# Degrees of a block by thirteen wide products and a masked sum, in the spread stage of a graph network kernel

## Chip, cores and metric

One core of a Trainium2 chip runs the whole program. The metric is device time in microseconds (us), from one launch. Engines: PE is TensorE (PEld its weight loads), DVE is VectorE, ACT is ScalarE, POOL is GpSimd, SP is SyncE, which here issues most DMAs.

## What is computed

Two graph layers on 6250 nodes and 206250 edges (100000 drawn ones in both directions and a self-loop per node, sorted by destination), each followed by a layer norm of the sum with its input. The first is attention with edge attributes and four heads of 64; the second is a pair of graph convolutions whose norm comes from the degrees:

```python
x = _layernorm(x + _L0_gnn_ref(x, edge_attr_64, W, att, bias, gamma, beta, edge_index))
# second layer, twice gcn_conv, then relu; x_out = _layernorm(x + that)
h = x @ W
deg = segment_sum(ones, dst, num_segments=n)
dinv = where(deg > 0, rsqrt(deg), 0.0)
norm = dinv[src] * dinv[dst]
out = segment_sum(h[src] * norm[:, None], dst, num_segments=n) + b
```

The degree of a node is the number of edges that end in it.

## The kernel before

The kernel is a row of stages, each a block of five instruction streams (one for each engine) that meet only in semaphores. The stage of this case is `spread_stage` (L734). It walks over the edges in 202 steps of 1024 edges (128 partitions, K = 8 each). Four steps make a block b, s = 0 to 3 is the step in it, and each has its own row buffer `rows[s]` (NR_BUF = 4). A step does two things.

*Edge rows.* PE turns the step's edge attributes in `turned` (`turn`, L1137), ACT copies them to SBUF (`evacuate`, L1089), PE multiplies them with the weights and adds a window of the source table (`product`, L1168 and L1174, in two halves), ACT takes the softplus (L1078, L1081), DVE weights the result with the attention vector and sums it up (`multiply` L1010, `add_up` L1019). Beside that, PE counts for every edge how many with the same block of source nodes stand before it (`count`, L1153 and eight products of L1156 into the bank `psr`, 450 columns and then 400, 350 and so on down to 50), and DVE turns these ranks into row numbers (`rank`, L967 to L978). POOL then writes the step's 1024 rows to DRAM, by eight indirect DMAs (`scatter`, L914): four when the first half's dot products are there, four when the second's are and when the next step's first product half is (`pre_ready[0]`, L918).

*Dense counts.* For the first 196 steps (blocks 0 to 48), the stage also builds the adjacency counts that the convolutions use. Each step handles a quarter of a block's destination lanes in four pieces q: DVE makes one-hots of columns (`columns`, L988) and lanes (`lanes`, L996), PE multiplies them (`adj`, L1185, three products of 392 columns), and ACT copies the sum to `cnts[u]` (`keep`, L1071). `cnts[u]` has 128 source lanes as partitions, and 49 chunks of 128 destination lanes; two of them alternate by block (u). At the end of a block ACT stores it with one DMA of 1568 KB.

The degrees of the 128 nodes of block b - 1 are the sum of its counts over source lanes and chunks. They are formed in block b. PE does it in `count` for step 1 of block b (`closes(b, s)`), ahead of the counting products: 49 products, one for each chunk, with the chunk as weights and one column of ones as the moving side, accumulated into one column of `psr`. `deg_ready` then lets DVE copy that column to `deg` (L972), in the middle of `rank` for step 1. ACT's first `keep` of a block waits for `deg_ready` too, since it writes the buffer that the degree products of one block earlier read.

PE's order in a step is written out by hand in `body` (L1189): adj 0, product half 0, adj 1, product half 1, turn of the next step, adj 2, count of the next step, adj 3. DVE's order (L1022): rank with columns and lanes of piece 1 in between, piece 2, one-hots and window mask of the next step, piece 3, multiply and add_up of both halves with the next step's piece 0 in between.

Of the kernel before, what the change touches and what calls it, by code (L numbers as in the profile page):

```python
# [15 lines left out]
fp32 = mybir.dt.float32  # L16
bf16 = mybir.dt.bfloat16
i32 = mybir.dt.int32
ALU = mybir.AluOpType
# [3 lines left out]
P = 128  # L23
# [22 lines left out]
CODE = 1024  # L46
TURN = 512
WIDE = 4
EXACT = 256
RANGE = 60.0  # L50
fp16 = mybir.dt.float16
# [682 lines left out]
def spread_stage(nc, z, m, sb, ps, sem, ea, att):  # L734
# [4 lines left out]
    with ExitStack() as ctx:  # L739
# [32 lines left out]
            "oh_ready", "ohT_made", "ranked", "summed", "idx_ready", "turned_ready", "evacuated"))  # L772
        pre_ready, exp_done, out_ready = ([sem(ctx, f"{n}S{h}") for h in range(2)] for n in (
            "pre_ready", "exp_done", "out_ready"))
        deg_ready = sem(ctx, "deg_ready")
        stored = [sem(ctx, f"adj_stored{u}") for u in range(2)]
        filled = sem(ctx, "filled_second")
        cut = z.groups[0] // NR_BUF
# [153 lines left out]
        def _(eng):  # L932
# [19 lines left out]
            def rank(b, s, h, between):  # L952

                t = step(b, s)
                j = s % 2
                count = Count()

                def own(ins, k):

                    ins.then_inc(v, count.up() and 1)  # L960
                    between(k)
                    eng.wait_ge(v, t * steps + count.n)

                wait(eng, sent[s], b * 16 * K)
                eng.tensor_copy(rows[s][:, :, LO:DOT], m["ends"][:, span(t * K, K), :])
                eng.wait_ge(ranked, t + 1)
                own(eng.tensor_tensor(  # L967
                    ranks[:, :, :], psr[:, 0:K * HB].rearrange("p (k h) -> p k h", h=HB),
                    m["base"][:, h, None, :].to_broadcast([P, K, HB]), ALU.add), 0)
                if closes(b, s):  # L970
                    eng.wait_ge(deg_ready, b)
                    eng.tensor_copy(m["deg"][:, span(b - 1, 1)], psr[:, (K + 1) * HB:(K + 1) * HB + 1])  # L972
                eng.tensor_tensor(m["base"][:, h, :], m["base"][:, h, :],
                                  psr[:, K * HB:(K + 1) * HB], ALU.add).then_inc(summed, 1)
                own(eng.tensor_tensor(ranks[:, :, :], ranks[:, :, :], oh[j][:, 0:K, :], ALU.mult), 1)
                assert count.n == steps
                with nc.allow_low_precision(reason="one whole number under 2**24 in each sum"):
                    eng.tensor_reduce(idx[s][:, :], ranks[:, :, :], AX.X, ALU.add).then_inc(idx_ready, 1)  # L978
# [36 lines left out]
            def add_up(b, s, part):  # L1015
# [3 lines left out]
                eng.tensor_reduce(rows[s][:, part * n:(part + 1) * n, DOT:DOT + DOTS], weighed[part][:, :, :, :], AX.X,  # L1019
                                  ALU.add).then_inc(dotted[part], 1)  # L1020

            def body(b, s, h=1):  # L1022
                nxt = later(b, s, 1)

                def between(k):
                    if dense(b):
                        (columns, lanes)[k](b, s, 1)

                rank(b, s, h, between)
                if dense(b):  # L1030
                    adj(b, s, 2)
                if exists(*nxt):
                    hots(*nxt)
                    windows(*nxt)
                if dense(b):
                    adj(b, s, 3)
                multiply(b, s, 0)
                if dense(nxt[0]):
                    columns(*nxt, 0)
                add_up(b, s, 0)  # L1040
                multiply(b, s, 1)
                if dense(nxt[0]):
                    lanes(*nxt, 0)
                add_up(b, s, 1)
# [4 lines left out]

            for j in range(2):  # L1050
                eng.memset(oh[j][:, K, :], 0.0).then_inc(cleared, 1)
            hots(0, 0)
            windows(0, 0)
            adj(0, 0, 0)
# [76 lines left out]
        def _(eng):  # L1131
            def turn(b, s):
                t = step(b, s)
                eng.wait_ge(ea_in[s % 2], ea_landed(b, s))
                wait(eng, evacuated, t)
                for g in range(K // 2):
                    mm = eng.transpose(turned[:, g, :], eaS[s % 2][:, 2 * g:2 * g + 2, :].rearrange("p k d -> p (k d)"), m["ident"][:, :])  # L1137
                mm.then_inc(turned_ready, 1)

            def count(b, s, u):  # L1140
                j = s % 2
                t = step(b, s)
                eng.wait_ge(oh_ready, t + 1)
                wait(eng, summed, t)
                if closes(b, s):
                    for q in range(GQ):
                        eng.wait_ge(copied[q], t - 1)
                    for c in range(NB):
                        mm = eng.matmul(psr[:, (K + 1) * HB:(K + 1) * HB + 1],
                                        cnts[1 - u][:, c, :, :].rearrange("p g d -> p (g d)"), m["onesb"][:, 0:1],  # L1150
                                        start=(c == 0), stop=(c == NB - 1), skip_group_check=True)
                    mm.then_inc(deg_ready, 1)
                eng.matmul(psr[:, 0:(K + 1) * HB], m["tri"][:, :], oh[j][:, :, :].rearrange("p k h -> p (k h)"),  # L1153
                           start=True, stop=False, skip_group_check=True)
                for d in range(1, K + 1):
# [5 lines left out]
            def product(b, s, h):  # L1161
# [13 lines left out]
                                        win[j][0:PW, :], start=False, stop=True, skip_group_check=True)  # L1175
                mm.then_inc(pre_ready[h], 1)

            def adj(b, s, q):
                t = step(b, s)
                r = q % 2  # L1180
# [8 lines left out]
            def body(b, s, u=None, after_u=1):  # L1189
# [9 lines left out]
                if u is not None:  # L1199
                    adj(b, s, 2)  # L1200
                if exists(*nxt):
                    count(*nxt, (after_u if u is None else u if s < NR_BUF - 1 else 1 - u))
                if u is not None:
                    adj(b, s, 3)

            def one(b, u):
                for s in range(NR_BUF):
# [5 lines left out]

            eng.wait_ge(cleared, 2)
            turn(0, 0)
            count(0, 0, 0)
            rounds(eng, NB // 2, two)
            if NB % 2:
                one(NB - 1, 0)
# [1913 lines left out]
```

## Time and profile before

| | us |
|---|---|
| median of 3 runs | 6543.93 |
| lowest and highest of them | 6538.44, 6555.55 |
| the profiled execution | 6502.53 |
| its span, first to last instruction | 6500.8 |
| spread stage in it, about | 301 to 3013 |

Over the whole span PE is busy 74%, DVE 75%, ACT 61%, POOL 62% of the time; the mean granted TensorE clock is 0.886 of full speed. The profiled execution is 41.4 us below the median of the runs. Stages follow each other with a barrier between them, so a us less in one stage is a us less in all. In the views below, "idle before" is the time in which the engine did nothing ahead of an instruction, followed by what ended it: an instruction of another engine, a DMA, "issue" (no semaphore update ended it) or "remote" (a semaphore update at whose time no sender's record ends).

### The profile page before, as it was taken

What the parts mean: (1) busy time and instruction counts of PE and PEld (TensorE: products, weight loads), DVE (VectorE), ACT (ScalarE), POOL (GpSimd) and SP (SyncE); (2) the same over time, 40 slices, a digit from 0 to 9 for tenths busy, and PEclk for the clock granted to TensorE, in tenths of its full rate; (3) what the DMA queues carried; (4) which work ended last, traced back from release to release, by engine and by line L of the source; (5) the groups of instructions that cost most, each with busy time, mean ns of one, the idle gap of its engine ahead of it and who ended that gap; (6) DMA issues with size and microseconds to landing.
All of it is one profiled execution on the core that took longest, in us unless ns stands there. A gap on an engine that the chain in (4) does not pass through costs nothing. (4 is left out here: it accounts for less than half of the span.)

```text
span 6500.8 us, 161934 instructions
## 1 busy us (share of the span) xinstructions
PE 4790.6 (74%) x32887; PEld 3107.1 (48%) x32888; DVE 4860.5 (75%) x21938; ACT 3979.7 (61%) x10577; POOL 4009.3 (62%) x5381
## 2 busy tenths in 40 slices
PE   1466666666666666664999999999938888886699
PEld 0233344334343433432555555555525556554699
DVE  6577777777677777773999999999976677777333
ACT  3355555555455545543999999999967777776100
POOL 1277777777677777764666666666627777776000
PEclk8588888878788778876999999999969999998799
DMA  8755556556455555555333333333317777775698
GB/s 224 239 186 182 186 193 197 184 191 194 160 188 174 175 170 167 176 162 160 72 72 72 72 73 74 73 73 73 73 37 216 217 217 223 213 219 174 258 360 344
DMA packets 1161941, 1090.82 MB, mean 168 GB/s; under 512 B 750004, under 2 KB 1023523, under 8 KB 1142980
## 3 DMA queue, kind: packets, MB, share of 16 engines
q1 hardware_dynamic: 1033656, 684.89, 38.9%
q0 software_dynamic: 88560, 320.26, 13.2%
q10 hardware_dynamic: 39580, 84.01, 3.4%
q8 instruction: 57, 0.93, 0.1%
q14 instruction: 88, 0.72, 0.0%
HBM read 658.14 MB, written 430.64 MB: 167 GB/s over the span
## 5 line engine op out<-in xcount | busy, mean ns | idle before, releaser
L914 POOL DMA_INDIRECT rows<-rowS,idx x1616 | 1949.0, 1206 | 787.9 <-issue 441.0
L1185 PE MATMUL psa<-one_c,one_s 128*128 128x392 bf16 x2352 | 605.1, 372 | 762.8 <-DVE one_s L996 461.4
L2425 PE MATMUL psm<-msg,onem 128*128 128x260 f32 x3648 | 918.0, 395 | 205.9 <-issue 169.7
L1694 DVE CUSTOM_DVE_ANT_0 junk<-bufh,attb 128x64 bf16<-128x64 f32 x5472 | 1043.5, 238 | 14.1 <-ACT bufh L1742 6.4
L2346 POOL TENSOR_TENSOR msg<-oj,heads 128x512 f32<-128x512 f32 x760 | 799.3, 1074 | 208.7 <-DMA oj<-rows 176.3
L988 DVE TENSOR_TENSOR one_c<-ioc,pairS 128x1176 bf16<-128x1176 f16 x784 | 598.4, 763 | 433.4 <-remote 227.7
L2425 PEld LDWEIGHTS psm<-msg,onem 128*128 128x128 f32 x3648 | 649.6, 190 | 474.0 <-issue 397.7
L1078 ACT ACTIVATE lgS<-preS 128x1024 f32<-128x1024 f32 x404 | 413.4, 1023 | 617.4 <-PE preS L1174 268.3
L1071 ACT ACTIVATE cnts<-psa 128x392 bf16<-128x392 f32 x784 | 366.8, 490 | 661.2 <-remote 344.3
L1782 PE MATMUL pre<-P3h,oneT 128*128 x5472 | 757.0, 275 | 0.0
L1659 POOL TENSOR_SCALAR one<-io128b,side 128x128 bf16<-128x128 bf16 x912 | 695.7, 763 | 67.2 <-DMA side<-rows 41.0
L2358 ACT ACTIVATE dist_m<-io,sums_lanes 128x128 f32<-128x128 f32 x1368 | 499.1, 396 | 292.4 <-PE psm L2425 265.1
L1185 PEld LDWEIGHTS psa<-one_c,one_s 128*128 128x128 bf16 x2352 | 211.0, 106 | 966.4 <-DVE one_s L996 640.4
L1667 POOL COPY eaC<-side 128x128 f32<-128x128 f32 x912 | 293.5, 322 | 572.0 <-PE turned L1769 565.7
L1777 PE MATMUL pre<-W2d,eaTh 64*128 64x256 f32 x3648 | 641.9, 429 | 0.0
L1782 PEld LDWEIGHTS pre<-P3h,oneT 128*128 128x128 bf16 x5472 | 460.9, 98 | 345.2 <-issue 303.0
L1738 ACT ACTIVATE lg<-pre 128x512 f32<-128x512 f32 x912 | 545.1, 598 | 111.2 <-PE pre L1782 110.5
L1168 PE MATMUL preS<-W2d,eaT 64*128 64x256 f32 x3232 | 590.0, 486 | 21.2 <-issue 19.0
L1742 ACT ACTIVATE bufh<-lg 128x512 f32<-128x512 f32 x912 | 574.6, 630 | 29.0
L1699 DVE CUSTOM_DVE_ANT_1 junk<-bufh,attb 128x128 bf16<-128x128 f32 x1824 | 560.6, 307 | 0.0
L2400 DVE TENSOR_TENSOR acc<-acc,psm 128x260 f32 x912 | 381.1, 418 | 108.3 <-DVE acc L2400 68.5
L1168 PEld LDWEIGHTS preS<-W2d,eaT 64*128 64x128 f32 x3232 | 346.3, 229 | 236.0 <-issue 201.4
(306 smaller groups left out, 9392.0 us busy)
## 6 DMA issues: line engine op xcount, KB each, us to landing
oj<-rows SPq DMA_DIRECT2D x912, 256.0 KB
adj<-adj SPq DMA_DIRECT2D x70, 1568.0 KB, 9.7
adj<-cnts ACTq DMA_DIRECT2D x49, 1568.0 KB
side<-rows SPq DMA_DIRECT2D x912, 69.0 KB, 2.3
bufh<-rows SPq DMA_DIRECT2D x912, 64.0 KB, 2.3
eaS<-in_edge_attr_dram SPq DMA_DIRECT2D x201, 256.0 KB
low<-dlow SPq DMA_DIRECT2D x202, 252.0 KB
adj_early<-adj SPq DMA_DIRECT2D x28, 1568.0 KB, 8.7
```

Source lines behind the costliest of these rows:

```text
L914: eng.indirect_dma_start(out=m["rows"][h], out_offset=bass.IndirectOffsetOnAxis(ap=idx[s][:, k:k + 1], axis=0), in_=rows[s][:, k, :], in_o ...
L988: eng.tensor_tensor(one_c[r][:, :, :].rearrange("p k (a w) -> p k a w", w=WIDE), m["ioc"][:, q, None, :].rearrange("p k (a w) -> p k a w", ...
L1168: eng.matmul(pre[h][:, q, a * C:(a + 1) * C], eaT[j][q * D:(q + 1) * D, 2 * h + a, :], m["W2d"][q * D:(q + 1) * D, :], start=(a == 0), sto ...
L1185: mm = eng.matmul(psa[r][:, 0:z.GC], one_s[r][:, k, :], one_c[r][:, k, :], start=(k == 0), stop=(k == GT - 1))
L1659: eng.tensor_scalar(one[j % PRE][:, 1, :], m["io128b"][:, :], side[j][:, 1, LANE - C:LANE - C + 1], 0.0, ALU.add, ALU.is_equal).then_inc(s ...
L1694: ins = eng.tensor_tensor_reduce(junk[q][:, k * H + h, 0, :], buf[j][:, k, 1, h * D:(h + 1) * D], attb[:, 1, h, :], 1.0, 0.0, ALU.mult, AL ...
L1699: ins = eng.tensor_tensor_reduce(junk[q][:, k * H + h, :, :], buf[j][:, k, :, h * D:(h + 1) * D], attb[:, :, h, :], 1.0, 0.0, ALU.mult, AL ...
L1742: eng.activation(buf[j][:, :, 1, 0:C], lg[q][:, :, :], ACT.Ln, bias=1.0).then_inc(sp_ready[j], 1)
L1777: eng.matmul(pre[j % PRE][:, k, 0:C], eaT[q][k * D:(k + 1) * D, :], m["W2d"][k * D:(k + 1) * D, :], start=True, stop=False, skip_group_che ...
L1782: mm = eng.matmul(pre[j % PRE][:, k, 0:C], oneT[q][:, k * P:(k + 1) * P], P3[:, bass.ds(b, 1), n, :].rearrange("p o c -> p (o c)"), start= ...
L2346: eng.tensor_tensor(msg[j][:, :, 0:C].rearrange("p k (h d) -> p k h d", h=H), oj[j][:, :, :, :], heads[:, :, j * UT:(j + 1) * UT].rearrang ...
L2425: mm = eng.matmul(psm[j][:, 0:C + H], one[q][:, k, :], msg[q][:, k, :], start=(k == 0), stop=(k == UT - 1))
```

## The change

The degree products leave `count` and become a function of their own, `degrees`, which PE runs in step 0 of a block after piece 3 of the counts. It takes the ones, all 128 x 128 of them, as weights and four chunks of counts as 512 moving columns, thirteen times (the last with one chunk), accumulated into the bank `turned`. Each partition of the bank then holds, for each of 128 destination lanes, the sums over source lanes, in four slots. Before it, PE waits until ACT has read the turned attributes of step 1 out of that bank, and the transposes of step 2 wait for DVE (`deg_read`). DVE multiplies the bank with the identity, which leaves each partition its own lane, and sums up the 512 columns; both stand behind `rank` in step 1, in place of the copy of one column. A tile `degm` of 128 x 512 fp32 and two semaphores are new, and the tile is cleared once.

```diff
+        degm = sb(ctx, "degm", [P, DEG, P], fp32)
 # DVE, rank()
-                if closes(b, s):
-                    eng.wait_ge(deg_ready, b)
-                    eng.tensor_copy(m["deg"][:, span(b - 1, 1)], psr[:, (K + 1) * HB:(K + 1) * HB + 1])
 # DVE
+            def degrees(b):
+                eng.wait_ge(deg_ready, b)
+                eng.wait_ge(deg_kept, b)
+                eng.tensor_tensor(degm[:, :, :], turned[:, :, :],
+                                  m["ident"][:, None, :].to_broadcast([P, DEG, P]), ALU.mult).then_inc(deg_read, 1)
+                eng.wait_ge(deg_read, b)
+                eng.tensor_reduce(m["deg"][:, span(b - 1, 1)], degm[:, :, :].rearrange("p c l -> p (c l)"), AX.X,
+                                  ALU.add).then_inc(deg_kept, 1)
 # DVE, body(), step 1 only
                 rank(b, s, h, between)
+                if closes(b, s):
+                    degrees(b)
 # PE, turn()
+                if s == 2 and (not isinstance(b, int) or 0 < b <= NB):
+                    eng.wait_ge(deg_read, b)
 # PE, count()
-                if closes(b, s):
-                    for q in range(GQ):
-                        eng.wait_ge(copied[q], t - 1)
-                    for c in range(NB):
-                        mm = eng.matmul(psr[:, (K + 1) * HB:(K + 1) * HB + 1],
-                                        cnts[1 - u][:, c, :, :].rearrange("p g d -> p (g d)"), m["onesb"][:, 0:1],
-                                        start=(c == 0), stop=(c == NB - 1), skip_group_check=True)
-                    mm.then_inc(deg_ready, 1)
 # PE
+            def degrees(b, u):
+                for q in range(GQ):
+                    eng.wait_ge(copied[q], NR_BUF * b)
+                eng.wait_ge(evacuated, NR_BUF * b + 2)
+                for c in range(0, NB, DEG):
+                    n = min(DEG, NB - c)
+                    mm = eng.matmul(turned[:, 0:n, :], m["onesb"][:, :],
+                                    cnts[u][:, c:c + n, :, :].rearrange("p c g d -> p c (g d)"),
+                                    start=(c == 0), stop=(c + n == NB), skip_group_check=True)
+                mm.then_inc(deg_ready, 1)
 # PE, body()
                 if u is not None:
                     adj(b, s, 3)
+                if s == 0 and (not isinstance(b, int) or 0 < b <= NB):
+                    degrees(b, 1 - (after_u if u is None else u))
```

## Rows read from the trace of the kernel before

**Rows 1.** Busy time of the engines in the spread stage (stage, us, busy, clock, DMA).

```profile
301.00:3013.00 2712.00, 1767.82 (x12165) 1063.17 (x12165) 1980.28 (x3819) 1397.61 (x2388) 1948.96 (x1616) 0.81 0.55 179
```

**Rows 2.** Groups by line, spread stage: executions, busy us, mean ns, idle before, its releasers.

```profile
L1010 DVE TENSOR_TENSOR weighed<-rowS,att_row 128x768 f32<-128x768 f32 x403 | 383.3, 951 | 61.3 <-ACT rowS L1081 43.4 <-issue 16.3
...
L967 DVE TENSOR_TENSOR ranks<-psr,base 128x400 f32<-128x400 f32 x201 | 113.9, 567 | 228.0 <-remote 199.6 <-PE psr L1156 28.4
...
L978 DVE TENSOR_REDUCE idx<-ranks 128x8 int32<-128x400 f32 x201 | 112.4, 559 | 0.2
...
L1149 PE MATMUL psr<-onesb,cnts 128*128 128x1 bf16 x2401 | 86.9, 163 | 100.9 <-issue 100.5
...
L972 DVE COPY deg<-psr 128x1 f32 x45 | 6.7, 150 | 0.0
```

**Rows 3.** Waits of POOL, spread stage: us in total, times, longest us.

```profile
POOL rows L914 <- issue: 441.0, 1420, 1.8
POOL rows L914 <- DVE rowS L1019: 126.4, 70, 5.5
POOL rows L914 <- ACT rowS L1092: 78.5, 57, 25.5
POOL rows L914 <- remote: 75.3, 34, 3.9
POOL rows L914 <- PE preS L1174: 66.3, 34, 9.1
```

**Rows 4.** Wait of DVE for its column one-hots, spread stage.

```profile
DVE one_c L988 <- remote: 227.7, 68, 10.7
```

**Rows 5.** Timeline of block 46: start us, length us, engine, line, operation, idle before.

```profile
2759.91 1.37 PE L1149 MATMUL psr<-onesb,cnts 128*128 128x1 bf16 x49
...
2761.32 0.93 PE L1156 MATMUL psr<-ohr,onesb 128*128 128x400 bf16 x8
...
2777.99 0.57 DVE L967 TENSOR_TENSOR ranks<-psr,base 128x400 f32<-128x400 f32 x1 [10.63 <-remote]
...
2779.02 1.05 POOL L914 DMA_INDIRECT rows<-rowS,idx  x1 [3.18 <-remote]
```

**Rows 6.** Timelines of PE, DVE and POOL in block 18, the longest pauses.

```profile
1243.42 0.47 PE L1149 MATMUL psr<-onesb,cnts 128*128 128x1 bf16 x13
...
1250.09 0.16 PE L1149 MATMUL psr<-onesb,cnts 128*128 128x1 bf16 x1 [1.25 <-issue]
...
1263.32 1.71 PE L1156 MATMUL psr<-ohr,onesb 128*128 128x400 bf16 x8
...
1265.06 0.57 DVE L967 TENSOR_TENSOR ranks<-psr,base 128x400 f32<-128x400 f32 x1 [9.96 <-PE psr L1156]
...
1269.12 1.45 POOL L914 DMA_INDIRECT rows<-rowS,idx  x1 [8.07 <-PE preS L1174]
```

**Rows 7.** Timelines of PE, ACT and DVE in block 44, undisturbed.

```profile
2649.38 1.37 PE L1149 MATMUL psr<-onesb,cnts 128*128 128x1 bf16 x49
...
2655.08 0.94 PE L1185 MATMUL psa<-one_c,one_s 128*128 128x392 bf16 x3 [2.85 <-DVE one_s L996]
...
2660.95 0.60 PE L1137 MATMUL turnedS<-ident,eaS 128*128 128x128 f32 x4
...
2650.85 0.58 ACT L1089 ACTIVATE eaT<-turnedS 128x512 f32<-128x512 f32 x1
...
2655.88 0.57 DVE L967 TENSOR_TENSOR ranks<-psr,base 128x400 f32<-128x400 f32 x1
...
2658.45 0.78 DVE L988 TENSOR_TENSOR one_c<-ioc,pairS 128x1176 bf16<-128x1176 f16 x1
```

**Rows 8.** DMA queues from 1240 to 1264 us: packets, MB, share.

```profile
q0 software_dynamic: 819, 2.83, 33.5%
q1 hardware_dynamic: 1341, 1.31, 19.8%
q10 hardware_dynamic: 128, 1.40, 14.4%
```

More of the change, by code:

```diff
@@ L48 @@
 WIDE = 4
+DEG = 4
 EXACT = 256
@@ L774, in spread_stage @@
             "pre_ready", "exp_done", "out_ready"))
-        deg_ready = sem(ctx, "deg_ready")
+        degm = sb(ctx, "degm", [P, DEG, P], fp32)
+        deg_ready, deg_read, deg_kept = (sem(ctx, n) for n in ("deg_ready", "deg_read", "deg_kept"))
         stored = [sem(ctx, f"adj_stored{u}") for u in range(2)]
@@ L1051, in _ @@
                 eng.memset(oh[j][:, K, :], 0.0).then_inc(cleared, 1)
+            eng.memset(degm[:, :, :], 0.0).then_inc(deg_kept, 1)
             hots(0, 0)
@@ L1138, in turn, with count @@
                 mm.then_inc(turned_ready, 1)
-            def count(b, s, u):
+            def count(b, s):
                 j = s % 2
@@ L1201, in body @@
                 if exists(*nxt):
-                    count(*nxt, (after_u if u is None else u if s < NR_BUF - 1 else 1 - u))
+                    count(*nxt)
                 if u is not None:
                     adj(b, s, 3)
+                if s == 0 and (not isinstance(b, int) or 0 < b <= NB):
+                    degrees(b, 1 - (after_u if u is None else u))
             def one(b, u):
@@ L1215, in _ @@
             turn(0, 0)
-            count(0, 0, 0)
+            count(0, 0)
             rounds(eng, NB // 2, two)
```

## The prediction, made before the changed kernel ran

> **What bounds the kernel now.** I read the views in the order in which the question narrows. First the busy time by stage: the spread stage, which holds the change, runs from 301 to 3013 us, and no engine is full there. DVE has the most busy time, POOL nearly as much, PE and ACT less, and the mean granted TensorE clock is 0.81 [rows 1]. So busy shares don't name the bound. The groups by line come next, for the durations of single operations [rows 2]. They stand beside the waits of each engine. POOL issues 1616 indirect DMAs, 1949 us, 1.21 us each [rows 1], and the waits of POOL add 441.0 us in 1420 gaps that end with "issue": 0.31 us between two of its instructions [rows 3]. That is 2390 of 2712 us. POOL waits for somebody only 346.8 us in all: DVE's dot products 126.4, ACT's copy of the edge rows 78.5 (25.5 of it once), PE's products 66.3, "remote" 75.3 [rows 3]. So POOL is the bound, and a change inside another engine is worth only what it changes in these 346.8 us or in POOL's own issue time.
>
> The degree products must therefore be read through the engines behind them. Forty-nine of them, with their weight loads, take 1.37 us when nothing disturbs them [rows 5, 7], 49 x 1.37 = 67 us in the stage. But the group has 100.9 us of idle time between its members, ended by "issue" [rows 2]. In the worst case that I looked at, the group begins at 1243.42 and the eight counting products behind it only at 1263.32, 19.9 us later, where an undisturbed block has 1.41 [rows 5]; between them PE stands up to 1.25 us for a single product, ended by "issue" [rows 6]. There is a second loss. DVE's first operation on the ranks, which reads the counting products, waits 199.6 us for "remote" and 28.4 us for PE [rows 2]. "Remote" is a semaphore update at which no sender's record ends. At 2759.91 the degree products and then the counting products end by the record at 2762.25, yet DVE, which needs the latter, starts at 2777.99 after 10.63 us idle, and POOL stands 3.18 us [rows 5]. Where neither happens, as at 2649.38, DVE starts its ranks right behind its own work with no idle time [rows 7]. What holds the updates back no row shows. I argue from the place: the long waits sit where DVE reads what PE made right behind the dense group of 98 PE instructions.
>
> **The change part by part.** *PE, removed.* 98 instructions in a burst become 26, and step 1's counting is no longer behind them. If the pauses and the late updates hang on the burst, 100.9 us of pauses and up to 228 us of DVE waiting can go. How much of it reaches POOL is read from the two disturbed blocks: 2.9 us of POOL's time beyond its usual 0.3 for 10.63 us of DVE's [rows 5], a share of 0.27; and 7.8 us for 18.5 us that the group was too long [rows 6], 0.42. The pauses and DVE's wait overlap (the wait is where the pauses end), so I count DVE's 228 us once, at the lower share, because slack swallows the short ones: 228 x 0.27 = 62 us. I take 50 of it, since some late updates come elsewhere too, where the burst is not near. The ends: nothing, if the cause is not the burst; and 141.6 us, all of POOL's waits for PE and "remote" [rows 3].
>
> *PE, added.* Thirteen products of 512 columns (the last of 128). Eight counting products with 1,800 columns in all take 0.93 us [rows 5], 0.52 ns a column, so 12 x 512 + 128 = 6,272 columns take 3.2 us; at the lower of the two clocks the eight took 1.71 us [rows 6], so 6.0 us. The Trainium skill, "TensorE: Matmul & The Clock Gate", section on matmul timing, gives 131 ns for a sustained and about 216 ns for an isolated product of 512 columns, 1.7 or 2.8 us in all, as an estimate; no row here has such a product, and either would be hidden like mine. The new group comes after the last accumulation of step 0 and before the first one of step 1. In the undisturbed block PE is idle there for 2.85 us, from 2652.23 to 2655.08, waiting for DVE's lanes [rows 7]; the counting, started 1.37 us earlier, adds to that, 4.2 us of cover. The new wait for ACT's copy of the turned tile costs at most 0.6 us of it: that copy ends at 2651.43, and PE's work before the new group would end at 2652.23 - 1.37 = 2650.86 [rows 7]. So 0.6 + 3.2 = 3.8 us fits into 4.2, and I cost it at nothing. At the lower clock it sticks out by 2.4 us; behind it wait the first accumulation of step 1, the products of step 1, and POOL, which holds its second half for those. The bound is 49 x 2.4 = 118 us at PE, times 0.27 is 32 us at POOL.
>
> *DVE.* The product with the identity and the sum are 128x512 fp32. From 128x400 at 567 ns to 128x768 at 951 ns is 1.04 ns an element, so 684 ns; the reduction of 128x400 took 559 ns, which gives 676 [rows 2]. The copy of 150 ns goes [rows 2]. Between the two DVE waits for its own result, some 0.1 us. That is 1.3 us a block, 64 us of DVE in the stage, in step 1, between the ranks and the one-hots for quarter 2. Queued behind it are the one-hots, the windows for step 2, and the weighed products that POOL waits for. DVE is not full (1980 of 2712 us [rows 1]), so by the same share, 0.27, 17 us reach POOL. Ends: nothing (DVE waits for ACT or a DMA right behind), and the whole 64 us. DVE's wait for the degree group itself is covered by the 2.6 us of its ranks (2655.88 to 2658.45 [rows 7]) and by what it does before them, unless PE is at the lower clock.
>
> *The turned bank.* The transposes of step 2 now wait for DVE's masked product. In the undisturbed block DVE would do it from 2658.45 to 2659.1, and PE turns step 2 at 2660.95 [rows 7]: covered by 1.8 us. Cost nothing; if the cover goes, the transposes shift by as much as DVE is late. The one memset is 0.5 us once. DMAs are not touched.
>
> *The sum.* -50 for the burst, +17 for DVE, 0 for the rest: -33 us. The profiled execution took 6502.53 us (span 6500.8), so it would take 6470; the median of the runs is 41.4 us above it, and I carry the same difference over: 6543.9 - 33 = 6511 us.
>
> **The rivals.** *The burst is not the cause (or the loss shows up behind the new group).* The pauses may come from what runs beside the group: the 1.6 MB store of the previous block's counts runs about then: 1.40 MB of its queue 10 fall into the window of the long pauses, and three queues together take 68% of the DMA engines' time [rows 8]. Then wide products or those after them pause as well, 26 instructions are exposed instead of 98, and a few us are won against DVE's 17: 6535 to 6560, say 6545. For it: DVE waits for "remote" at its column one-hots as well, 227.7 us in 68 places [rows 4], so late updates aren't bound to the ranks. Against: in both disturbed blocks the long wait stands at the first thing that DVE needs from behind the degree group [rows 5, 6]. The Trainium skill, "Runtime: NRT & Kernel Launch", section "Instruction fetch mechanics", says that instructions are fetched in 16 KiB blocks, and that a taken branch to a page outside the window stalls the engine; by that rule the pauses would be code loading, they would move with the loop and not with the burst, and the time would be about this rival's. The window of the long pauses has packets of queues 0, 1 and 10 and none of an instruction queue [rows 8], so the trace speaks against code loading.
>
> *DVE becomes the late one, the slower side.* POOL already waits 126.4 us in 70 places for DVE's dot products [rows 3]. If in step 1 POOL mostly stands at that wait, every us on DVE ahead of it counts: 64 us in full, and half of it where slack remains. Without a gain from the burst that is 6544 + 32 to 64, say 6580. It decides from the point where DVE's added 1.3 us exceed its lead over POOL in step 1.
>
> *The whole loss goes.* All of POOL's waits for PE and "remote", 141.6 us, less DVE's 17: 6544 - 125 = 6419 us.
>
> **How the numbers follow.** Forecast 0.43 (own range 6480 to 6530), burst not the cause 0.28, DVE late 0.23, whole loss 0.06. The predicted time is the forecast's, 6511. The range of 8 in 10 reaches from 6455, which takes in part of the larger gain, to 6580, the price of the slower rival. A measurement of this kernel can tell about 0.3%, 20 us, from no change. Faster by more: the forecast and the whole loss, 0.49, less a little of the forecast's edge, 0.47; within: 0.30; slower: 0.23.
>
> **What the profile would show.** The degree group would have 13 members, 3.2 us long, no pauses; DVE's ranks would wait for "remote" under 60 us in place of 199.6; POOL's waits for PE and "remote" would fall from 141.6 to under 90; DVE's busy time would rise by 64 us; POOL's waits for DVE would rise by less than 20 us. The forecast is wrong if the "remote" waits stay, or if they go and POOL's share of "DVE rowS" takes their place.

## The result and the profile after

The changed kernel takes 6488.92 us, median of 5 runs (6482.48 to 6512.39), against 6542.47 (6523.25 to 6555.55, 5 runs) for the kernel before on the same chip. The ratio is 0.9928, 95% interval 0.9900 to 0.9956: 53 us less by the medians, 47 by the ratio, 29 to 65 by the interval. A second comparison (after_again, below) gave 0.9937 (0.9914 to 0.9959).

The profiled execution of after took 6488.92 us, that of before 6502.53, only 13.6 us apart: before's was a short one of its kind, 40 us under its median, and after's is its median. So the two traces understate the gain, and I read from them what waits for whom, not the size.

The stage as a whole, in the columns of [rows 1]:

```profile
300.00:2994.00 2694.00, 1791.77 (x10352) 1037.88 (x10401) 2047.70 (x3867) 1395.28 (x2387) 1898.29 (x1616) 0.83 0.54 180
```

It is shorter by 18 us (2694 from 2712). DVE's busy time rose by 67 us, from 1980.28, where 64 were costed. The groups that answer to [rows 2], lines of the changed file (group | busy us, mean ns | idle before, its releasers):

```profile
L1191 PE MATMUL turnedS<-cnts,onesb 128*128 128x512 bf16 x539 | 149.6, 434 | 87.0 <-ACT eaT L1101 60.2 <-issue 26.7
...
L969 DVE TENSOR_TENSOR ranks<-psr,base 128x400 f32<-128x400 f32 x201 | 114.1, 568 | 47.0 <-remote 47.0
...
L1191 PEld LDWEIGHTS turnedS<-cnts,onesb 128*128 128x128 bf16 x637 | 65.1, 107 | 177.5 <-issue 129.3
...
L1025 DVE TENSOR_TENSOR degm<-turnedS,ident 128x512 f32<-128x512 f32 x49 | 33.5, 683 | 32.9 <-remote 26.0 <-issue 6.4 <-PE turnedS L1191 0.4
```

The product with the identity took 683 ns (684 estimated). DVE's wait for remote at the ranks went from 199.6 to 47.0 us; a part came back in front of the new product, 26.0 us. The new PE group is a matter of its own: it waits 60.2 us for ACT's copy of the turned tile. The waits of POOL, against [rows 3]:

```profile
POOL rows L916 <- issue: 456.3, 1439, 1.8
POOL rows L916 <- DVE rowS L1018: 187.1, 89, 5.4
POOL rows L916 <- remote: 85.9, 38, 3.5
POOL rows L916 <- ACT rowS L1104: 61.2, 26, 25.3
POOL rows L916 <- PE preS L1180: 29.6, 24, 3.6
```

PE and remote together fell from 141.6 to 115.5 us, and DVE's dot products rose from 126.4 to 187.1. All waits that aren't "issue" make 363.8 us, not less than the 346.8 of before. What fell is POOL's own time: 1949 to 1898 us for the same 1616 DMAs.

An undisturbed block of after, PE and then DVE (start us, length us, idle before), against [rows 7]:

```profile
1420.01 0.93 PE L1162 MATMUL psr<-ohr,onesb 128*128 128x400 bf16 x8
1420.79 0.66 PE L1203 MATMUL psa<-one_c,one_s 128*128 128x392 bf16 x3
1422.22 2.59 PE L1191 MATMUL turnedS<-cnts,onesb 128*128 128x512 bf16 x12 [0.78 <-ACT eaT L1101]
1428.27 1.16 PE L1203 MATMUL psa<-one_c,one_s 128*128 128x392 bf16 x3 [3.46 <-issue]
...
1435.17 0.60 PE L1151 MATMUL turnedS<-ident,eaS 128*128 128x128 f32 x4
```

```profile
1429.06 0.57 DVE L969 TENSOR_TENSOR ranks<-psr,base 128x400 f32<-128x400 f32 x1
...
1431.57 0.68 DVE L1025 TENSOR_TENSOR degm<-turnedS,ident 128x512 f32<-128x512 f32 x1
1432.40 0.69 DVE L1028 TENSOR_REDUCE deg<-degm 128x512 f32 x1
1433.01 0.76 DVE L987 TENSOR_TENSOR one_c<-ioc,pairS 128x1176 bf16<-128x1176 f16 x1
```

The counting products are done before the degree group starts. Twelve records of the thirteen products take 2.59 us (this trace lacks one in every block, 588 of 637), PE waits 0.78 us for ACT ahead of it and stands another 3.46 us behind it before the next accumulation, DVE finds it ready, and PE's transposes at 1435.17 come well after DVE's product at 1431.57. That is the picture of the forecast.

### The profile page after: what moved, and what is told of

Its sections match the earlier page's. It is cut to its first block and busy times, and to the rows that moved or that the text cites. A ratio compares the mean times of both kernels' runs of the same rounds, so it can differ in the third digit from the quotient of the medians.

```text
span 6487.2 us, 158407 instructions
## 1 busy us (share of the span) xinstructions
PE 4811.6 (74%) x31074; PEld 3081.9 (48%) x31124; DVE 4925.9 (76%) x21988; ACT 3976.5 (61%) x10577; POOL 3947.5 (61%) x5381
## 5 line engine op out<-in xcount | busy, mean ns | idle before, releaser
L916 POOL DMA_INDIRECT rows<-rowS,idx x1616 | 1898.3, 1175 | 820.2 <-issue 456.3
L1714 DVE CUSTOM_DVE_ANT_0 junk<-bufh,attb 128x64 bf16<-128x64 f32 x5472 | 1057.4, 241 | 15.3 <-ACT bufh L1762 6.6
L987 DVE TENSOR_TENSOR one_c<-ioc,pairS 128x1176 bf16<-128x1176 f16 x784 | 600.6, 766 | 478.1 <-remote 319.0
L1174 PE MATMUL preS<-W2d,eaT 64*128 64x256 f32 x3232 | 575.5, 481 | 29.7 <-issue 27.8
```

The lines of the kernel that those rows point to most:

```text
L916: eng.indirect_dma_start(out=m["rows"][h], out_offset=bass.IndirectOffsetOnAxis(ap=idx[s][:, k:k + 1], axis=0), in_=rows[s][:, k, :], in_o ...
L987: eng.tensor_tensor(one_c[r][:, :, :].rearrange("p k (a w) -> p k a w", w=WIDE), m["ioc"][:, q, None, :].rearrange("p k (a w) -> p k a w", ...
L1174: eng.matmul(pre[h][:, q, a * C:(a + 1) * C], eaT[j][q * D:(q + 1) * D, 2 * h + a, :], m["W2d"][q * D:(q + 1) * D, :], start=(a == 0), sto ...
L1714: ins = eng.tensor_tensor_reduce(junk[q][:, k * H + h, 0, :], buf[j][:, k, 1, h * D:(h + 1) * D], attb[:, 1, h, :], 1.0, 0.0, ALU.mult, AL ...
```

## The experiments

Differences in us are the ratio times the time of the kernel before. Three theories were to be told apart. A: the burst of 98 PE instructions makes PE pause and its updates come late, wherever it stands. B: it is the place, since step 1's counting no longer stands behind the group. C, added after the second set: the wide DVE operations themselves make the gain. All ratios are to the kernel before, run in between on the same chip, with the 95% interval in brackets. "Surroundings" stands for whatever differs between the sets without being in the program; it is told by the time of the kernel before.

### First set: surroundings in which nothing comes late

*The narrow group at the new place.* From the changed kernel, where DVE's product and sum give way to the copy of one column:

```diff
-                for c in range(0, NB, DEG):
-                    n = min(DEG, NB - c)
-                    mm = eng.matmul(turned[:, 0:n, :], m["onesb"][:, :],
-                                    cnts[u][:, c:c + n, :, :].rearrange("p c g d -> p c (g d)"),
-                                    start=(c == 0), stop=(c + n == NB), skip_group_check=True)
+                for c in range(NB):
+                    mm = eng.matmul(turned[:, 0, 0:1], cnts[u][:, c, :, :].rearrange("p g d -> p (g d)"),
+                                    m["onesb"][:, 0:1], start=(c == 0), stop=(c == NB - 1), skip_group_check=True)
...
-                eng.tensor_tensor(degm[:, :, :], turned[:, :, :],
...
-                eng.tensor_reduce(m["deg"][:, span(b - 1, 1)], degm[:, :, :].rearrange("p c l -> p (c l)"), AX.X,
...
+                eng.tensor_copy(m["deg"][:, span(b - 1, 1)], turned[:, 0, 0:1]).then_inc(deg_read, 1)
```

> The 49 narrow products stay as they are, but stand where the change puts its wide ones (step 0, behind piece 3 of the counts), write one column of the turned bank, and DVE copies that column behind its ranks; no wide DVE operation. The degrees are computed in full. Theory A (the burst of 98 PE instructions holds PE's updates back, wherever it stands): the loss moves to what is behind it, 6520 to 6550 us, and the pauses inside the group stay near 100 us. Theory B (it is the place: the counting of step 1 no longer stands behind the group, and DVE gets its ranks in time): the whole gain of the change or more, since DVE is spared its 1.3 us a block, 6465 to 6490 us, DVE's wait at the ranks for remote near the changed kernel's 47 us.

Measured: ratio 1.0005 (0.9952 to 1.0058), with the kernel before at 6185.41 us.

*The wide group at the old place.* From the kernel before, in `count`, and DVE's copy goes to a scratch tile:

```diff
-                    for c in range(NB):
-                        mm = eng.matmul(psr[:, (K + 1) * HB:(K + 1) * HB + 1],
-                                        cnts[1 - u][:, c, :, :].rearrange("p g d -> p (g d)"), m["onesb"][:, 0:1],
-                                        start=(c == 0), stop=(c == NB - 1), skip_group_check=True)
+                    for c in range(0, NB, 4):
+                        n = min(4, NB - c)
+                        mm = eng.matmul(psr[:, 0:n * P], m["onesb"][:, :],
+                                        cnts[1 - u][:, c:c + n, :, :].rearrange("p c g d -> p c (g d)"),
+                                        start=(c == 0), stop=(c + n == NB), skip_group_check=True)
...
+            eng.memset(m["deg"][:, :], 33.0)
```

> The group stays at the old place ahead of step 1's counting, but as thirteen wide products into the ranks' own bank; DVE copies one column of it to a scratch tile and the degrees are a constant 33, so the degrees are left out and only the products' time is kept. Theory A (burst): 26 instructions don't hold anything back, the gain of the change comes without its DVE operations, 6465 to 6490 us, DVE's wait at the ranks for remote under 70 us. Theory B (place): the group is 3 us long in place of 1.4 and still ahead of the counting, so nothing is won, 6540 to 6560 us, and the wait stays near 200 us.

Measured: ratio 1.0044 (0.9997 to 1.0090).

*The narrow group twice.*

```diff
-                    for c in range(NB):
+                    for c in [*range(NB), *range(NB)]:
```

> The kernel before with the group of 49 products run twice in a row at its old place (the second run starts the sum anew, so the degrees are the same). Theory A (burst): 196 instructions; the pauses of 100 us and the late updates at least double, 6585 to 6640 us. Theory B (place, by the time that the group takes undisturbed): 1.2 us more a block ahead of the counting, 60 us at PE, 0.27 of it at POOL, 6555 to 6565 us.

Measured: ratio 1.0020 (0.9966 to 1.0073).

*No degrees.* The 49 products, `deg_ready` and DVE's copy are taken out of the kernel before, and `deg` is set to 33.

> The kernel before without degree products and without DVE's copy; the degrees are a constant 33, so they are left out. It is the most that any form of the degree work can win in this stage. Both theories: at or below the changed kernel, 6450 to 6485 us. The difference to the changed kernel (6489) is what its wide products and two DVE operations still cost: 17 us by the forecast. POOL's waits for PE and remote together (141.6 us before) under 100 us if the degree group made them.

Measured: ratio 0.9969 (0.9918 to 1.0019).

None of the four moved, and none of the expected times was met, neither A's nor B's. But theory A is not refuted by it, because what it is about isn't there: the kernel before itself ran at 6185 us, 357 us faster than in the comparison of the result. The trace of narrow_twice shows the surroundings: first two groups by line, then POOL's waits.

```profile
L914 POOL DMA_INDIRECT rows<-rowS,idx x1616 | 1934.0, 1197 | 518.4 <-issue 478.4 <-ACT rowS L1092 28.4 <-DVE rowS L1019 10.4
...
L1149 PE MATMUL psr<-onesb,cnts 128*128 128x1 bf16 x4802 | 127.2, 163 | 2.1 <-issue 2.0
```

```profile
POOL rows L914 <- issue: 478.4, 1569, 0.3
POOL rows L914 <- ACT rowS L1092: 28.4, 9, 26.0
POOL rows L914 <- DVE rowS L1019: 10.4, 34, 0.3
POOL rows L914 <- PE preS L1174: 1.2, 4, 0.3
```

4802 products pause for 2.1 us in all, where 2401 paused for 100.9 [rows 2]. DVE's ranks wait for nobody, no engine's wait in the stage is ended by remote, and POOL, which stood 346.8 us, stands 40.0. The stage ends at 2728 us with twice the products, in place of 3013. The DMA engines are not emptier (share 0.61 in this stage against 0.55 in [rows 1]), and the store of the counts runs there as well (its queue 10 moves 78.68 MB in the stage in both traces). The row of the stage, in the columns of [rows 1]:

```profile
301.00:2728.00 2427.00, 1759.43 (x14566) 1101.82 (x14566) 1983.97 (x3818) 1404.17 (x2388) 1934.00 (x1616) 0.84 0.61 200
```

One thing in these traces limits what a releaser's name is worth. In the stage, the trace of before holds 23,451 records of semaphore updates, that of narrow_twice 54,399, and that of narrow_twice_2 (third set, the same program as narrow_twice, where updates come late) 23,462. Where updates come late, more than half of the records are missing. The idle times stand, since they come from the instructions' own records; that a wait is put down to remote, to issue or to a certain engine is less sure there.

### Second set: the surroundings of the result again, and the parts

*The changed kernel again.*

> The changed kernel again. On a chip or at a time where PE's updates come late and PE pauses inside the group (kernel before at 6542 us), it should win 0.5 to 1.0%, as before. Where neither is there, as in the four runs so far (kernel before at 6185 us, POOL waiting for nobody), the theory that all of the gain is made of these two losses says a ratio of 0.998 to 1.003; a theory that the counting's earlier place is worth something by itself says 0.993 there too.

Measured: 6443.13 against 6484.53 us, 0.9937 (0.9914 to 0.9959). It fell into surroundings with late updates, so its second half, a quiet chip, wasn't tried.

*The kernel before again.*

> The kernel before, unchanged, for its trace in the same surroundings and for the size of an apparent difference where there is none: ratio 0.997 to 1.003. If it runs at about 6185 us, DVE's ranks wait for remote under 10 us and the degree group pauses under 10 us, in place of 199.6 and 100.5; if it runs at about 6540 us, both are back.

Measured: 6476.50 us, 0.9991 (0.9973 to 1.0008): no difference where there is none. Its trace, beside that of after_again, is a second pair. Groups and waits of before_again:

```profile
L914 POOL DMA_INDIRECT rows<-rowS,idx x1616 | 1915.7, 1185 | 788.8 <-issue 450.2 <-DVE rowS L1019 144.5 <-ACT rowS L1092 77.4
...
L967 DVE TENSOR_TENSOR ranks<-psr,base 128x400 f32<-128x400 f32 x201 | 114.1, 568 | 101.0 <-remote 88.8 <-PE psr L1156 8.1 <-issue 4.0
...
L1149 PE MATMUL psr<-onesb,cnts 128*128 128x1 bf16 x2401 | 84.7, 164 | 88.6 <-issue 87.9
```

```profile
POOL rows L914 <- DVE rowS L1019: 144.5, 69, 4.7
...
POOL rows L914 <- remote: 74.6, 33, 4.1
POOL rows L914 <- PE preS L1174: 41.8, 31, 8.9
```

and of after_again:

```profile
L916 POOL DMA_INDIRECT rows<-rowS,idx x1616 | 1953.6, 1209 | 724.3 <-issue 461.1 <-DVE rowS L1018 142.5 <-remote 50.8
...
L1191 PE MATMUL turnedS<-cnts,onesb 128*128 128x512 bf16 x588 | 148.5, 407 | 58.8 <-ACT eaT L1101 43.8 <-issue 14.9
...
L969 DVE TENSOR_TENSOR ranks<-psr,base 128x400 f32<-128x400 f32 x201 | 114.1, 568 | 32.4 <-remote 31.8 <-issue 0.6
```

```profile
POOL rows L916 <- DVE rowS L1018: 142.5, 80, 5.9
POOL rows L916 <- remote: 50.8, 31, 3.7
...
POOL rows L916 <- PE preS L1180: 22.1, 17, 9.3
```

Here POOL's waits for PE and remote fall from 116.4 to 72.9 us, its waits for DVE stay (144.5, 142.5), and its own time rises from 1915.7 to 1953.6. In the first pair it was the other way round. So the split of POOL's time into waits and longer DMAs isn't stable from one execution to the next, and the names of the waits rest on incomplete records. DVE's wait for remote at its columns rose from 227.7 [rows 4] to 319.0 in the first pair and fell from 305.8 to 297.5 in the second. What both pairs share is that the ranks' wait falls (199.6 to 47.0, 88.8 to 31.8) and that the pauses between PE's degree products fall (100.5 to 26.7, 87.9 to 14.9).

*DVE's part alone.* Added to the kernel before:

```diff
                 rank(b, s, h, between)
+                if closes(b, s):
+                    eng.wait_ge(deg_kept, b)
+                    eng.tensor_tensor(degm[:, :, :], degs[:, :, :],
+                                      m["ident"][:, None, :].to_broadcast([P, 4, P]), ALU.mult).then_inc(deg_read, 1)
+                    eng.wait_ge(deg_read, b)
+                    eng.tensor_reduce(degx[:, :], degm[:, :, :].rearrange("p c l -> p (c l)"), AX.X,
+                                      ALU.add).then_inc(deg_kept, 1)
```

> The kernel before with the changed kernel's two wide DVE operations (a product of 128x512 with the identity and its sum) added behind the ranks of step 1, on a tile of zeros in SBUF; the result is not used and the degrees are computed as before. It prices DVE's part alone. By my share of 0.27: 17 us, ratio 1.003. The rival (DVE in full): 64 us, ratio 1.010. Where POOL waits for nobody: 0 us, ratio 1.000.

Measured: 6454.64 us, 0.9957 (0.9936 to 0.9978). More work made the kernel faster, which neither expectation allowed for. The two operations took what was costed, the groups being

```profile
L917 POOL DMA_INDIRECT rows<-rowS,idx x1616 | 1863.8, 1153 | 845.0 <-issue 454.6 <-DVE rowS L1022 189.2 <-PE preS L1186 74.8
...
L1161 PE MATMUL psr<-onesb,cnts 128*128 128x1 bf16 x2401 | 99.3, 164 | 146.4 <-issue 146.0
...
L1038 DVE TENSOR_REDUCE degx<-degm 128x1 f32<-128x512 f32 x49 | 33.6, 686 | 1.7
L1035 DVE TENSOR_TENSOR degm<-degs,ident 128x512 f32<-128x512 f32 x49 | 33.5, 683 | 0.0
```

and POOL's DMAs took 1153 ns each in place of 1185 in before_again, while its idle time rose from 788.8 to 845.0 us. 45 us of that are waits for DVE (189.2 from 144.5), as a load on DVE would give; the kernel is faster in spite of them. The degree group, which the edit leaves alone, paused for 146.4 us in this trace, against 88.6 in before_again, so the sum of the pauses in one trace doesn't tell the kernel's time. With the two operations the edit also brings three tiles and two semaphores; these weren't tried alone. Why it is faster is open.

*One operation for product and sum.* In the changed kernel:

```diff
-                eng.tensor_tensor(degm[:, :, :], turned[:, :, :],
-                                  m["ident"][:, None, :].to_broadcast([P, DEG, P]), ALU.mult).then_inc(deg_read, 1)
-                eng.wait_ge(deg_read, b)
-                eng.tensor_reduce(m["deg"][:, span(b - 1, 1)], degm[:, :, :].rearrange("p c l -> p (c l)"), AX.X,
-                                  ALU.add).then_inc(deg_kept, 1)
+                eng.tensor_tensor_reduce(degm[:, :, :], turned[:, :, :],
+                                         m["ident"][:, None, :].to_broadcast([P, DEG, P]), 1.0, 0.0, ALU.mult, ALU.add,
+                                         degx[:, :]).then_inc(deg_read, 1)
+                eng.wait_ge(deg_read, b)
+                eng.tensor_copy(m["deg"][:, span(b - 1, 1)], degx[:, :]).then_inc(deg_kept, 1)
```

> The changed kernel with DVE's product and sum made in one operation (and a copy of one column): some 0.85 us of DVE a block in place of 1.37, the degrees in full. A version that could beat both. By the share of 0.27 it wins 49 x 0.52 x 0.27 = 7 us over the changed kernel, ratio to the kernel before lower by 0.001; where POOL waits for nobody, no difference to the changed kernel.

Measured: 6432.53 us, 0.9922 (0.9899 to 0.9945). The one operation took 683 ns, the reading of its sum 83 and the copy 154, 0.92 us a block where 0.85 were expected. It is faster than the kernel before; whether it is faster than the changed kernel (6443.13, 0.9937) can't be told, the intervals overlap almost wholly.

### Third set: burst, place and ceiling, where updates come late

The kernels of the first set, with the kernel before at 6492.69 us.

> The narrow group at the new place with DVE's copy of one column, as in narrow_new_place, in the hope of surroundings with late updates (kernel before at 6450 us or more); ratios to the kernel before there. Theory A (burst): 0.997 to 1.003, and the pauses inside the group stay near 90 us. Theory B (place): 0.990 to 0.995 with DVE's wait for remote at the ranks near 40 us, pauses or not. Theory C (the gain comes from the two wide DVE operations, which alone gave 0.9957): 0.998 to 1.003, since there are none. In quiet surroundings 1.000 again.

Measured: 6465.17 us, 0.9960 (0.9940 to 0.9981).

> The wide products at the old place, DVE's copy of one column only, degrees left out (a constant 33), as in wide_old_place. With late updates about: theory A (burst): 0.990 to 0.996, DVE's wait for remote at the ranks under 50 us. Theory B (place): 1.000 to 1.004, since the group is longer and still ahead of the counting. Theory C: 0.998 to 1.003. In quiet surroundings 1.000 to 1.005 again.

Measured: 6454.40 us, 0.9935 (0.9914 to 0.9957).

> The narrow group twice at its old place, as in narrow_twice. With late updates about: theory A (burst): 1.006 or more, pauses inside the group about 200 us in place of 88 to 100. Theory B (place, undisturbed length): 1.001 to 1.004. Theory C: the same as B. In quiet surroundings 1.002 again.

Measured: 6578.64 us, 1.0147 (1.0116 to 1.0179).

> No degree products and no copy, degrees left out (a constant 33), as in no_degrees: the ceiling. With late updates about: theories A and B: 0.985 to 0.993, at or below the changed kernel's 0.9928 and 0.9937. Theory C: 0.998 to 1.001, since DVE's operations, which would make the gain, aren't there. In quiet surroundings 0.997 again.

Measured: 6425.71 us, 0.9899 (0.9870 to 0.9928).

The groups of degree products and ranks in narrow_twice_2, wide_old_place_2 and narrow_new_place_2, in this order, with DVE's copy of the degree column in the last:

```profile
L1149 PE MATMUL psr<-onesb,cnts 128*128 128x1 bf16 x4802 | 180.8, 164 | 228.6 <-issue 226.9
...
L967 DVE TENSOR_TENSOR ranks<-psr,base 128x400 f32<-128x400 f32 x201 | 114.4, 569 | 301.4 <-PE psr L1156 151.7 <-remote 148.8 <-issue 0.8
```

```profile
L1152 PE MATMUL psr<-cnts,onesb 128*128 128x512 bf16 x588 | 138.3, 381 | 12.0 <-issue 11.8
...
L968 DVE TENSOR_TENSOR ranks<-psr,base 128x400 f32<-128x400 f32 x201 | 114.2, 568 | 51.8 <-remote 51.6
```

```profile
L969 DVE TENSOR_TENSOR ranks<-psr,base 128x400 f32<-128x400 f32 x201 | 114.1, 567 | 35.4 <-remote 32.6 <-issue 2.7
...
L1185 PE MATMUL turnedS<-onesb,cnts 128*128 128x1 bf16 x2401 | 85.2, 164 | 133.3 <-issue 93.0 <-ACT eaT L1096 39.6
...
L1024 DVE COPY deg<-turnedS 128x1 f32 x45 | 7.0, 155 | 123.0 <-remote 108.1 <-issue 9.6 <-PE turnedS L1185 5.4
```

Twice the burst gives 228.6 us of pauses, where the single one had 100.9, 88.6 and 146.4 in three traces (before, before_again, narrow_and_dve), and 95 us more on the kernel (75 to 116), though the undisturbed group is only 1.2 us longer a block, 60 us at PE; in the first set the same edit gave 1.0020, its interval including 1. Wide products at the old place, without any wide DVE operation, pause for 12.0 us, and bring 42 us; the ranks wait 51.6 us for remote, just above the 50 that A had set. So theory C falls as the cause of the gain, and A holds.

The narrow group at the new place brings 26 us, about half of what the change brings. It keeps its pauses (93.0 us by issue, 39.6 of its 133.3 for ACT). DVE's ranks wait only 35.4 us, but the wait has moved more than gone: the copy of the degree column, which now stands behind the ranks, waits 123.0 us (and 4.3 more in the four copies listed apart), 163 us for both, where the ranks alone waited 101.0 and 228.0 in the two traces of before. So B isn't enough as a rival, and the place has a worth of its own as long as the products are narrow; that it comes from DVE getting its ranks in time isn't shown. Theory A had said 0.997 to 1.003 for it, theory B 0.990 to 0.995; the interval lies between them and touches both. With wide products the place adds nothing that can be seen: 0.9935 at the old place without the wide DVE operations, 0.9928 and 0.9937 at the new one with them.

A rival without a run of its own is the granted clock. In the stage it is 0.84 in wide_old_place_2 and 0.83 and 0.85 in the two traces of the changed kernel, against 0.81 and 0.82 in the two traces of before, so a part of what wide products bring may be clock. It can't be the whole. The kernel without degree products gained the most at 0.81:

```profile
302.00:2919.00 2617.00, 1676.40 (x9764) 993.40 (x9764) 1992.32 (x3770) 1396.21 (x2389) 1834.79 (x1616) 0.81 0.56 186
```

And in the first set wide_old_place had 0.87, narrow_twice and no_degrees 0.84, and it was not faster (1.0044).

With no degree products 66 us are gained (47 to 84).

POOL's waits in no_degrees_2 show what the ceiling doesn't remove:

```profile
POOL rows L914 <- DVE rowS L1016: 214.3, 86, 5.7
POOL rows L914 <- remote: 72.7, 34, 4.0
...
POOL rows L914 <- PE preS L1166: 13.5, 21, 5.6
```

The waits on PE's products fall to 13.5 us, but 72.7 us of remote stay with no degree product in the kernel, and DVE's grow to 214.3. DVE's column one-hots wait 326.4 us for remote there, more than in before (227.7 [rows 4]). Late updates are there without the burst, so it isn't their only source.

## Why the prediction was right or wrong

*Sign and size.* 33 us were forecast, 47 and 41 came by the ratios of the two comparisons (53 and 41 by the medians), and 33 lies in both intervals. The measured 6489 lies in the range.

*What bounds the stage.* That POOL does was borne out by the quiet surroundings: 1934.0 us of DMAs and 478.4 of gaps in a stage of 2427, with 40 us of waits (26 of them before the first DMA). But "POOL's waits are what can be won" was too simple. Its DMAs stretch from 1135 ns (no_degrees_2: 1834.8 us for 1616) to 1209 (after_again), and the gain of the first pair stands in that column, not in the waits.

*The burst, -50.* Right. Wide products in its place brought 42 us, and the most that the whole group can give is 66 us; the 62 that came out of 228 us times the share of 0.27 from one block was close to it. That share was taken from a single block and could have been off by half; the trace of before_again has only 101 us of ranks' waits in place of 228, at nearly the same kernel time, so the agreement owes something to luck.

*PE, added, 0.* The products came close to what was costed. At the full clock they were a little cheaper: all thirteen are in the record of after_again, in 2.81 us against my 3.2:

```profile
1411.58 2.81 PE L1191 MATMUL turnedS<-cnts,onesb 128*128 128x512 bf16 x13 [0.56 <-ACT eaT L1101]
```

The twelve records in after took 2.59, so one product of 512 columns counts 0.22 us. Over all blocks the group is busy for 151.3 us in after_again, 3.1 us a block, since in some the clock is lower (in the block of after shown next twelve records take 3.75 us, with a granted clock of 0.71 from 2714.9 to 2719). The Trainium skill, "TensorE: Matmul & The Clock Gate", section "Back-to-back issue gap", has about 216 ns for isolated products of this width, with which that agrees, and 131 ns for sustained ones, which isn't seen here. The mis-sized term is the wait for ACT's copy. I allowed 0.6 us of it from an undisturbed block, hidden; PE waits for it 60.2 us in 27 blocks, up to 7.00 us:

```profile
2714.99 3.75 PE L1191 MATMUL turnedS<-cnts,onesb 128*128 128x512 bf16 x12 [7.00 <-ACT eaT L1101]
2718.57 0.66 PE L1203 MATMUL psa<-one_c,one_s 128*128 128x392 bf16 x3
```

ACT was late itself there: it stood 5.95 us, ended by remote, before the softplus in front of that copy, and made the copy at 2713.89. A wait that is covered in an undisturbed block isn't covered in a disturbed one. What it cost the kernel wasn't run alone.

*The place, 0.* I gave the earlier counting no value of its own, except as cover. It brought 26 us with the burst unchanged, so a term was missing; beside wide products no value of it shows.

*DVE, +17.* The durations were right (683 and 686 ns, 67 us in all), the price on the kernel was not: added alone they gave -28 us (interval -14 to -42) where +17 was forecast. So the terms don't add up as I had them. Measured one by one, 42 for the wide form, 26 for the place and 28 for DVE's operations would make 96 us, but the change brought 41 to 47, and leaving out the degree work altogether 66. That the sum of -50 and +17 came out near the result is in part luck. From 66 us without degree work to 41 or 47 with the change, 19 to 25 us are still paid for the wide products, the wait for ACT and DVE together. These are differences of ratios whose intervals overlap, so they bound the rest, they don't price it.

*The signs in the profile.* The ranks' wait under 60 us: yes, 47.0 and 31.8. Thirteen members without long pauses: yes. DVE's busy time up by 64: 67 in the first pair, 54 in the second (2040.85 from 1986.85). POOL's waits for PE and remote under 90 us: no in the first trace (115.5), yes in the second (72.9). POOL's waits for DVE up by less than 20 us: no, 61, and yes, -2. By my own sign of being wrong (POOL's waits for DVE take the place of the remote ones) the first pair spoke against the forecast and the second for it, with the same gain. The sign was worth little, because it hangs on names of waits in single traces.

*The rivals.* That the burst isn't the cause is refuted by its doubling (1.0147) and by the wide products at the old place. Its own cause, the store beside the group, isn't enough by itself: it runs in quiet surroundings too, and nothing pauses there. I had also read [rows 8] too coarsely. All 128 packets of queue 10 in that window lie between 1240 and 1244 us, and the pauses run from 1244 to 1263, when that queue has none. The slower side, DVE as the late one, is refuted by narrow_and_dve, whose kernel time fell. Code loading, the reading that went with the first rival, is spoken against once more: narrow_twice is the same program, with the same loops and the same code, in both sets, and its pauses make 2.1 us in one and 228.6 in the other, with the same 18 packets of instruction queue 8 in the stage. The whole loss could not go: 66 us is all that hangs on the degree group, not 125.

What makes PE pause and its updates come late was not found. It is of the surroundings: narrow_new_place, wide_old_place, narrow_twice and no_degrees ran at 6167 to 6221 us once and at 6426 to 6579 us another time, under the same chip number; the second set had another number, with the kernel before at 6485. What the change is worth in quiet surroundings wasn't run; the parts that were (0.9969 for no degrees at all, its interval including 1) leave at most some 0.8% and speak for nearly nothing.

## What to carry to other kernels

Ask of a group of small operations not what they take, but what stands behind them in the queue and who waits for that. Here groups of 49 products, 1.37 us each when undisturbed, cost 66 us of kernel time in all. Their 67 us of undisturbed PE time lie beside other engines' work, and in quiet surroundings leaving them out gave no difference that could be told (0.9969, its interval including 1). Test such a cause by doubling it and by changing its form in place, and look first whether the disturbance is there at all in the surroundings of the test: the first set told nothing about it, because nothing came late there and the kernel before was about 5% faster. When a wait goes from one reader, look at the next reader behind it before you call it gone: the ranks' 35 us in narrow_new_place_2 went with 127 us at the copy behind them. Don't read a difference of 1% off one pair of traces: two traces of the same kernel differed by 111 us in the very wait on which the forecast rested.

## What the hardware showed that I had not expected

- Readers of PE's results can start long after the product that they need has ended by the record. In block 46 of before the counting ends at 2762.25 and DVE's ranks start at 2777.99 [rows 5], 15.7 us later, of which DVE stood 10.63. ACT, which waits for PE's accumulations, starts within 0.04 us of DVE:

```profile
2778.03 0.89 ACT L1071 ACTIVATE cnts<-psa 128x392 bf16<-128x392 f32 x2 [14.71 <-remote]
```

  The degree group of that block ran through in 1.37 us, so late updates come without pauses too.
- PE can stop for 0.4 to 1.25 us between single products, in a window (1240 to 1264 us) without a packet of an instruction queue [rows 6, 8]. In other surroundings that makes 2.1 us in 4802 products, and no wait in the stage ends by remote.
- The kernel before took 6185 us in one set and 6493 us in another. The difference lies nearly all in this stage: in narrow_new_place, which ran in both, it ended at 2697 us once and at 2987 (narrow_new_place_2) the other time.
- Work added to an engine that isn't the bound, 67 us on DVE, made the kernel 0.2 to 0.6% faster. No cause was found.
